# Two-layer graph transformer: layer 1 run over three groups at once, with its transposes taken from TensorE to VectorE and DRAM

## The reference

```
x = layernorm(x + L0(x, adj))     # 8 heads of 48, attention, rmsnorm, SiLU MLP 384-1536-384, rmsnorm
x = layernorm(x + L1(x, adj))     # 12 heads of 32, attention only
L0:  q,k,v = x@wq+bq, x@wk+bk, x@wv+bv
     p = softmax(q k^T * 48**-0.5 + adj);  ctx = p v;  x1 = rms(x + ctx@wo + bo)*alpha1 + gamma1
     out = rms(x1 + silu(x1@w1 + b1)@w2 + b2)*alpha2 + gamma2
```

## Time and profile before

| | us |
|---|---|
| median of 3 runs | 2070.93 (2070.71 to 2072.68) |
| the profiled execution | 2069.64 |
| its span | 2067.8 |
| PE busy | 2028.7 (98%) |
| PE weight loads busy | 1940.5 (94%) |
| DVE busy | 1306.6 (63%) |
| ACT busy | 1137.7 (55%) |
| POOL busy | 514.5 (25%) |

### The profile page before, as it was taken

One profiled execution on the slowest core, in us unless ns is written; L12 is line 12 of the kernel. 1 busy time (PEld: TensorE's weight loads), 2 busy tenths in 40 slices (PEclk: granted clock), 3 DMA queues, 4 the chain that ended last, 5 costly groups with the idle time before them and its releaser, 6 DMA issues.

```text
span 2067.8 us, 46600 instructions
## 1 busy us (share of the span) xinstructions
PE 2028.7 (98%) x16832; PEld 1940.5 (94%) x16832; DVE 1306.6 (63%) x2430; ACT 1137.7 (55%) x2400; POOL 514.5 (25%) x625
## 2 busy tenths in 40 slices
PE   6999999999999999999999999998999999999997
PEld 6999999999999999999999999998899999999997
DVE  6655556655556655556655556655777767776775
ACT  6555555555555555545555555554556555655565
POOL 4223232223232223232223232222122212221221
PEclk9999999999999999999999999999999999999999
DMA  7122121122121121121121121122222222222221
GB/s 215 36 58 54 43 58 43 47 59 52 43 58 43 47 61 50 43 58 43 47 62 48 43 58 43 47 59 78 68 81 84 61 81 82 81 63 81 83 77 63
DMA packets 218876, 129.49 MB, mean 63 GB/s; under 512 B 129888, under 2 KB 217696, under 8 KB 218848
## 3 DMA queue, kind: packets, MB, share of 16 engines
q1 hardware_dynamic: 218848, 129.12, 23.1%
HBM read 78.40 MB, written 37.75 MB: 56 GB/s over the span
## 4 chain that ended last, share of the span: by engine, by line
PE 96%; DVE 2%; ACT 1%; DMA 0%; issue 0%; POOL 0%; SPq 0%; ACTq 0%; POOLq 0%; DVEq 0%
PE a_bank L328 59%; PE b_bank L1092 15%; PE b_banks L1092 5%; PE b_banks L1132 4%; PE a_bank L377 4%; PE b_bank L1155 2%; PE a_bank L404 2%; PE b_banks L1142 2%; PE a_bank L390 1%; PE b_bank L1165 1%; PE a_bank L414 1%; PE a_bank L431 1%; DMA a_work<-in_L_gnn_w 0%; DMA a_work<-in_L_gnn_wq 0%; DVE a_work L705 0%
## 5 line engine op out<-in xcount | busy, mean ns | idle before, releaser
L727 DVE TENSOR_TENSOR a_hid_lo<-a_work,a_hid_hi 128x512 fp32r<-128x512 f32 x192 | 146.6, 763 | 376.7 <-ACT a_hid_hi L573 376.7
L328 PE MATMUL a_bank<-a_x1t_hi,a_w_hi 128*128 128x256 f32 x1152 | 328.1, 285 | 1.5 <-DVE a_x1t_lo L713 1.5
L328 PE MATMUL a_bank<-a_x1t_lo,a_w_hi 128*128 128x256 f32 x1152 | 322.3, 280 | 0.0
L328 PE MATMUL a_bank<-a_x1t_hi,a_w_lo 128*128 128x256 f32 x1152 | 322.0, 280 | 0.0
L568 ACT ACTIVATE a_work<-a_bank,a_b 128x256 f32<-128x256 f32 x384 | 161.1, 472 | 283.5 <-PE a_bank L328 282.3
L919 POOL TENSOR_TENSOR a_work<-a_work,a_gamma 128x384 f32<-128x384 f32 x128 | 150.5, 1197 | 588.4 <-DMA a_work<-in_x 564.0
L328 PE MATMUL a_bank<-a_w_hi,a_hid_hi 128*128 128x384 f32 x768 | 264.1, 344 | 0.5 <-DVE a_hid_lo L727 0.5
L328 PE MATMUL a_bank<-a_w_lo,a_hid_hi 128*128 128x384 f32 x768 | 258.2, 336 | 0.0
L328 PE MATMUL a_bank<-a_w_hi,a_hid_lo 128*128 128x384 f32 x768 | 258.2, 336 | 0.0
L328 PEld LDWEIGHTS a_bank<-a_x1t_hi,a_w_hi 128*128 128x128 f32 x1152 | 217.8, 189 | 5.5 <-DVE a_x1t_lo L713 1.7
L328 PEld LDWEIGHTS a_bank<-a_x1t_lo,a_w_hi 128*128 128x128 f32 x1152 | 217.8, 189 | 0.0
(11 more groups left out here) (157 smaller groups left out, 5698.5 us busy)
## 6 DMA issues: line engine op xcount, KB each, us to landing
a_work<-in_x SPq DMA_DIRECT2D x64, 384.0 KB, 3.4
a_work<-in_xT SPq DMA_DIRECT2D x96, 128.0 KB, 2.6
x2T<-a_z_blocks SPq DMA_DIRECT2D x256, 48.0 KB, 1.7
x<-a_work SPq DMA_DIRECT2D x32, 384.0 KB, 2.7
b_xt_raw<-x2T SPq DMA_DIRECT2D x32, 384.0 KB, 3.5
b_res<-x SPq DMA_DIRECT2D x32, 384.0 KB, 3.8
out<-b_normed SPq DMA_DIRECT2D x32, 384.0 KB, 2.5
b_v_pairs<-b_v_nat SPq DMA_DIRECT2D x128, 49.5 KB, 2.0
```

Of the source, the lines that this page charges most:

```text
L328: r = pe.matmul(out, lhs[a], rhs[b], start=first and n == 0, stop=last and n == 2)
L727: dve.tensor_tensor(hid[1][:, p % RING, :], silu[:, p % 2, :], hid[0][:, p % RING, :].bitcast(F32), ALU.subtract).then_inc(hid_lo, 1)
```

## The change

The layer's step handles three groups instead of two: in step(g), g is new (scores, exp), b = g-1 is back (PV, output projection, x1) and f = g-2 is in the feed-forward; the final norm is of e = g-3. PV of b is issued first on PE, right ahead of the scores of g.

- All 20 PE transposes per group are removed. Instead DVE transposes P, ctx and x1 in 32x32 blocks (turn_p, turn_ctx, turn_x1), SP stores the blocks to a DRAM scratch with eight DMAs of 32 partitions each, and one DMA loads them back in their new place; ACT then makes the hi half (or the copy of P) and DVE the lo half from SBUF.
- exp is written in two pieces per tile into pt, and the copy back from prob to pt is two pieces per tile. The addition of gamma1 goes from POOL to DVE.
- The blocks of ctx, x1 and the output are interleaved so that each SBUF row of a store is 4 runs of 96 values (384 bytes), those of P 4 runs of 128 values (512 bytes). x2T has the same block layout, and the rows of wo, w1 and the second layer's Wq, Wk, Wv are loaded in the order that fits (by_block).
- To make room, w1 is staged in two slots of 512 columns (three pieces) and w2 in two slots of one row block (twelve pieces); eight of the twelve w2 pieces are split in step 0 and four in step 1.
- In the second layer only the layout of its transposed input changes, and its first split (xt_high(0), xt_low(0)) now stands ahead of last["scalar"][0]() and last["vector"][0]().

The core of the diff:

```diff
-            def store(g):
-                for t in range(TILES):
-                    sp.wait_ge(turned, TILES * g + t + 1)
-                    for b in range(P // 32):
-                        sp.dma_start(x2T[g, t, b], z_blocks[32 * b:32 * b + 32, t, :].rearrange("p (k c) -> p k c", c=32)).then_inc(
-                            x2t_stored, 16)
+            def store_p(g, t):
+
+                sp.wait_ge(p_turned, TILES * g + t + 1)
+                for s in range(P // 32):
+                    sp.dma_start(scratch["p"][s, t], prob[32 * s:32 * s + 32, t, :].rearrange("p (u c) -> p u c", u=4)).then_inc(
+                        p_stored, 16)
+
+            def load_pt(g):
+                sp.wait_ge(p_stored, 16 * N_TURNED * (g + 1))
+                sp.dma_start(v["p"], scratch["pt"]).then_inc(pt_loaded, 16)
+
+            def store_blocks(src, dst, t, stored):
+                for s in range(P // 32):
+                    sp.dma_start(dst[P // 32 * t + s], src[32 * s:32 * s + 32, t, :].rearrange("p (m c) -> p m c", m=4)).then_inc(
+                        stored, 16)
+
+            def store_ctx(g, t):
+                sp.wait_ge(ctx_turned, TILES * g + t + 1)
+                store_blocks(blocks, scratch["ctx"], t, ctx_stored)
+
+            def load_ctxt(g):
+                sp.wait_ge(ctx_stored, 16 * N_TURNED * (g + 1))
+                sp.dma_start(turned_raw, scratch["ctxt"]).then_inc(ctxt_loaded, 16)
+
+            def store_x1(g, t):
+                sp.wait_ge(x1_turned, TILES * g + t + 1)
+                store_blocks(blocks, scratch["x1"], t, x1_stored)
+
+            def load_x1t(g):
+                sp.wait_ge(x1_stored, 16 * N_TURNED * (g + 1))
+                sp.dma_start(turned_raw, scratch["x1t"]).then_inc(x1t_loaded, 16)
+
+            def store_x2(g):
                 sp.wait_ge(res_done, TILES * (g + 1))
                 sp.dma_start(x2[g], z).then_inc(x2_stored, 16)
 
+            def store_x2t(g):
+                for t in range(TILES):
+                    sp.wait_ge(z_turned, TILES * g + t + 1)
+                    store_blocks(z_blocks, x2T[g], t, x2t_stored)
+
...
+
+            def load_w2(which):
+                for i in which:
+                    if i >= len(w2_slots):
+                        sp.wait_ge(w2_lo, i - len(w2_slots) + 1)
+                    sp.dma_start(w2_slots[i % len(w2_slots)], w["w2"][i * P:(i + 1) * P, :]).then_inc(
+                        w2_loaded[i % len(w2_slots)], 16)
...
+                if back:
+                    for t in range(TILES):
+                        store_ctx(b, t)
+                if nxt:
+                    load_adj(g + 1)
+                if back:
+                    load_ctxt(b)
...
+                if new:
+                    load_pt(g)
+                if first:
+                    sp.wait_ge(w1_lo, N_W1)
+                if new and (nxt or back):
+                    load_x(g)
+                if first:
+                    load_w2(range(2, 10))
+                if back:
+                    for t in range(TILES):
+                        store_x1(b, t)
+                if late:
+                    store_x2(e)
+                if back:
+                    load_x1t(b)
+                if back and not ffn:
+                    load_w2(range(10, FC))
+                if late:
+                    store_x2t(e)
+                if ffn:
+                    load_res(f)
+                if ffn and not new and back:
...
                 if isinstance(g, int) and g == 0:
                     pe.wait_ge(w_lo, WO + 1)
-                pe.wait_ge(ctxt_lo, TILES * g + t + 1)
                 if t == 0:
-                    pe.wait_ge(ctx_done, TILES * g + 2)
+                    pe.wait_ge(ctxt_lo, g + 1)
+                    pe.wait_ge(ctx_done, TILES * (g + 1))
+                elif new:
+                    pe.wait_ge(biased, TILES * (g + 1) + 1)
...
+            def step(g, new=True, nxt=True, back=True, ffn=True):
+                b, f = g - 1, g - 2
+                if back:
+                    for t in range(TILES):
+                        pv(b, t, new)
+                if new:
+                    for t in range(TILES):
+                        scores(g, t, back)
+                if nxt and not ffn:
                     qk(g + 1)
                 if ffn:
+                    for p in range(3):
+                        ffn1(f, p, new)
                     ffn2(f, 0)
-                    ffn1(f, 2, att)
-                    ffn1(f, 3, att)
+                    ffn1(f, 3, new)
                     ffn2(f, 1)
-                if att:
-                    for t in range(TILES):
-                        turn_p(g, t)
+                    ffn1(f, 4, new)
+                if back:
+                    for t in range(TILES):
+                        attn_out(b, t, new)
                 if ffn:
                     ffn2(f, 2)
-                if att:
-                    for t in range(TILES):
-                        pv(g, t)
-                if ffn:
-                    ffn1(f, 4, att)
-                    ffn2(f, 3)
-                if att:
-                    for t in range(TILES):
-                        turn_ctx(g, t)
-                if ffn:
-                    ffn1(f, 5, att)
-                if att:
-                    for t in range(TILES):
-                        attn_out(g, t)
-                if ffn:
-                    ffn2(f, 4)
-                    ffn2(f, 5)
-
-            step(0, ffn=False)
-            step(1)
-            with pe.Fori(2, NG - 1) as g:
+                    ffn1(f, 5, new)
+                    for p in range(3, FP):
+                        ffn2(f, p)
+                if nxt:
+                    if ffn:
+                        qk(g + 1)
+                    for t in range(TILES):
+                        values(g + 1, t)
+
...
+            def take_pt(g, t):
+                act.wait_ge(pt_loaded, 16 * (g + 1))
+                for s in range(2):
+                    half_t = slice(256 * s, 256 * s + 256)
+                    r = act.activation(pt[:, t, half_t].rearrange("p (h q j) -> p h q j", q=2, j=32),
+                                       prob[:, t, half_t].rearrange("p (q h j) -> p h q j", q=2, j=32), ACT.Copy)
+                r.then_inc(pt_done, 1)
...
+            def ctxt_high(g):
+                act.wait_ge(ctxt_loaded, 16 * (g + 1))
+                wait(act, o_mm, TILES * g)
+                act.activation(ctx_t[0][:].rearrange("p k (n j) -> p k n j", j=32),
+                               turned_raw.rearrange("p (n k j) -> p k n j", k=KT, j=32), ACT.Copy).then_inc(ctxt_hi, 1)
...
+                    for t in range(TILES):
+                        exp(g, t)
+                if first:
+                    high(pieces[WO], w_loaded[WO], 64, w_hi)
+                    for i in range(2):
+                        w1_high(i)
+                if ffn:
+                    hidden(f, 1)
+                if nxt and not first:
+                    split_x(g + 1)
+                if ffn:
+                    hidden(f, 2)
+                    hidden(f, 3)
+                if back:
+                    ctxt_high(b)
+                if not new and ffn and not back:
+                    for i in range(2):
+                        high(next_pieces[i], next_loaded[i], 64, next_hi)
+                if late:
                     variance(e)
                 if ffn:
...
+                    hidden(f, 4)
...
+                if new:
+                    for t in range(TILES):
+                        take_pt(g, t)
+                if back and not second:
+                    x1t_high(b)
+                if nxt:
+                    for u in (1, 2):
+                        take_q(g + 1, u)
+                if first:
+                    w1_high(2)
+                    w2_high(range(0, 8))
+                if second:
+                    w2_high(range(8, FC))
+                    x1t_high(b)
...
+            def turned_low(dst, hi, done, n):
+                dve.wait_ge(hi, n)
+                dve.tensor_tensor(dst[1][:].rearrange("p k (n j) -> p k n j", j=32),
+                                  turned_raw.rearrange("p (n k j) -> p k n j", k=KT, j=32),
+                                  dst[0][:].bitcast(F32).rearrange("p k (n j) -> p k n j", j=32),
+                                  ALU.subtract).then_inc(done, 1)
...
+            def turn_p(g, t):
+                dve.wait_ge(exp_done, TILES * g + t + 1)
+                dve.transpose(prob[:, t, :], pt[:, t, :]).then_inc(p_turned, 1)
+
...
+            def turn_ctx(g, t):
+                dve.wait_ge(ctx_done, TILES * g + t + 1)
+                if t == 0:
+                    wait(dve, x1_stored, 16 * N_TURNED * g)
+                dve.transpose(blocks[:, t, :], ctxt[:, t, :]).then_inc(ctx_turned, 1)
...
+                for t in range(TILES):
+                    dve.wait_ge(x1_scaled, TILES * g + t + 1)
```

(83 more changed lines are left out.)

730 lines of the change are left out of this document (325 added, 405 removed).

## The result

The changed kernel takes 2076.61 us (median of 9 runs, 2075.2 to 2078.24), the kernel before 2071.69 in runs beside it. The ratio is 1.0024, 95% interval 1.0014 to 1.0034: slower by about 5 us. Forecast were 2081 and slower, with a range of 2053 to 2104. The profiled execution's span is 2074.2 us, before 2067.8.

What follows compares the result with a forecast made beforehand. TensorE (PE), busy for 98% of the span, was taken to bound the kernel. From the profile's time, 2069.64 - 70 + 22 + 46 + 13 = 2080.6, forecast as 2081 us; range 2053 to 2104.

Steps and rivals of the forecast that it cites:

- transposes off TensorE: First layer: removing three transposes from TensorE saves 2.19 us a group, 70 us for 32 groups.
- wait for ctx lo: Loop, ahead of attn_out: TensorE waits 0.8 us in 28 steps, 22 us; F is the step's first ffn1 pair's start.
- start: Ahead of the first ffn1, which would start at 110: 46 us more idle, from 33 to 58.
- end and seam: Last two groups and passage to the second layer: waits and half clock together 22 us, 13 more than now.
- second layer: Layer behind the seam: left as it is, no term in the sum.
- Rival 1: Loop at ctx: VectorE's queue is 0.8 shorter, no wait, the 22 goes, 2059 us; chance 0.22.
- Rival 2: Start: 10 to 13 us cheaper than laid out, time about 2069, no change; chance 0.13.
- Rival 3: Loop: VectorE's norm runs beside GpSimd's additions, each step 1.3 longer, 36 us, 2117; chance 0.05.
- Rival 4: DRAM detours: stores and loads take twice as long, 14 us in the loop, 2110 at most; chance 0.15.

Runs made afterwards that it cites:

- experiment 3: Changed kernel with the split of the next x moved behind the split of ctx on ScalarE and VectorE, norm left in place: 2048.15 us, ratio 0.9877.
- experiment 5: Kernel of experiment 3 with twenty extra TensorE transposes per group in one block ahead of attn_out: 2112.91 us, one run.
- experiment 6: Kernel of experiment 3 with twenty extra TensorE transposes per group in three blocks: 2116.18 us, one run.
- experiment 2: Changed kernel with the norm behind ctx's lo half on VectorE, its squares and root behind those of x1 on ScalarE and GpSimd: 2053.15 us, ratio 0.991.
- experiment 4: Changed kernel with eight extra TensorE transposes per group directly ahead of attn_out: 2081.17 us, one run.
- experiment 7: Changed kernel with the first P's return issued ahead of the ten constant loads on SyncE at the start: 2070.82 us, ratio 0.9988.
- experiment 8: Changed kernel with w2 staged in six slots instead of two and the start's pieces and loads reordered: 2053.22 us, ratio 0.9902.
- experiment 9: Kernel of experiment 8 with x(0) loaded early, behind the first two parts of w1: 2049.07 us, ratio 0.9892.
- experiment 1: Changed kernel with the second norm of group e moved behind ctx's lo half on VectorE alone: 2073.11 us, ratio 1.000.
- experiment 12: Kernel of experiments 3 and 9 plus an earlier second-layer first load, with the last group's attn_out ahead of the fifth ffn1 pair: 2012.63 us, ratio 0.9713.

## Why the prediction was right

The sum, in us of span; the measured start is 108.58 - 51.21 = 57.4, less the 13.5 of moved work that the prediction took off.

| term | forecast | measured | from |
|---|---|---|---|
| transposes off TensorE | -70 | -80 | 32 x 2.50, experiment 3 |
| wait for ctx lo | +22 | +27.4 | 28 x 0.98, experiment 3 |
| start | +46 | +44 | first ffn1 |
| end and seam | +13 | +14 | what the other rows leave of the 6.4 |
| second layer | 0 | +0.8 | |
| sum | +11 | +6.4 | spans |

The 2.50 is the loop's value, taken for all 32 groups. The start's 44 takes over the forecast's 13.5 of moved work. TensorE is idle there for 55.5 us against 18.1 before, 37.4 more; the other 6.5 are work at a lower clock. The end's 14 is no measurement of its own. Its rows give 9.7 of idle time and some 5 of slow clock, which agrees to about 1 us; the estimate adds 1.7 and 2.7 for the last two groups and 0.9 for the second layer's first matmuls (8.78 against 7.84).

- *What bounds the kernel, and that TensorE's queue is gained in full:* right, but the sizing was short. The rows of the three transposes gave 2.19 a group; the removal was worth 2.50. This is the term that was mis-sized, by 10 us. The step that failed is "This is the whole gain: projections, scores and PV keep their number and shape". They do, but in their new places they take 0.56 less (experiments 5 and 6), and the transposes, measured by starts, 1.93.
- *The wait at attn_out:* right in place, releaser, count and cause. Forecast / measured, from F: norm starts 11.1 / 11.2, ctx lo starts 14.6 / 14.8, TensorE 15.6 / 15.7. TensorE came 0.1 later than laid out and was free 0.1 earlier (at 14.7), which made 0.98 of 0.8. Experiments 2 and 3 show that split and norm make it together: without the norm 0.16 is left of it, without the split nothing. Experiment 4 shows that 0.87 us of other work on TensorE fit into it.
- *Rival 1* (no wait at ctx) is what experiment 3 makes. It needs 0.9 us, and no closeness of starts gave that. The rival's 2059 would have been 2048 with the right price of the transposes.
- *Rival 2* (a start cheaper by 10 to 13): it was 2 cheaper.
- *Rival 3* (the norm meets GpSimd): not there. The norm's four instructions keep their length, since GpSimd's additions end at F+2.
- *Rival 4* (the detour shows): not in the loop. ScalarE took ctx at F+13.0, SyncE had issued its load at 797.94, F+5.7. The Trainium skill ("DMA: Bandwidth & Descriptors", Specifications) asks for 512 bytes or more for line rate. The time to landing here shows no price for less (1.7 us at 384 bytes); what rate the stores could reach, no run here shows.
- *The start*, forecast / measured: P back 46 / 44.8, ctx(0) 70.4 / 68.1, q and k of group 2 79 / 75.7, end of attn_out 90 / 87.7, first ffn1 110 / 108.6. Experiments 7 to 9 confirm the reasons (constants ahead of P; w2 in two slots ahead of ctx), and that 26 of the 44 are queue order and slots, without telling the two apart.
- *The end*, forecast / measured: waits 4.3 and 5.2 / 3.4 and 4.9, seam 10.2 / 10.3. The slow clock behind them cost more than the 1.3 taken: 54 ffn1 matmuls need 6.4 in the loop and took 8.1 and 9.1. The granted clock was 0.57 over the first 3.9 us behind the first wait, and 0.50 over 3.8 behind the second.

The two mis-sized terms, 10 and 5 us, had opposite signs. That the forecast of 2081 came within 5 us of the time is in part luck.

## What to carry to other kernels

Work taken off the engine that bounds a kernel is gained in full only while the others have slack at the next hand-over: lay out the instructions between what this engine releases and what it next waits for, with their durations, and look which of them do not belong to that hand-over (here a norm and a split, 3 us of 13). When one is moved, move what reads it on every other engine too; experiments 1 and 12 moved one engine's half and got the wait back at another place. What happens once, at the start and the end, can cost more than 32 groups save: 58 us there stood against 53 net in the loop.

## What was not expected of the hardware

Twenty transposes in one block cost 2.02 us, where the three blocks' rows in the kernel before add up to 2.19 and their removal with the new order gave 2.50. The same 12 ffn2 matmuls take 2.08 or 2.25 by what stands ahead of them. Such neighbours are worth half a microsecond a group here, and the rows of the removed instructions don't contain that. And VectorE's subtraction L789 took 1.50 instead of 0.69 when GpSimd's additions ran beside it, as the norm had before the change:

```profile
835.02 1.98 POOL L985 TENSOR_TENSOR a_work<-a_work,a_bo 128x384 f32<-128x384 f32 x2
...
836.06 1.50 DVE L789 TENSOR_TENSOR a_work<-a_work,a_smax 128x512 f32<-128x512 f32 x1
...
838.91 0.69 DVE L789 TENSOR_TENSOR a_work<-a_work,a_smax 128x512 f32<-128x512 f32 x1
```

The meeting that rival 3 feared exists, at another instruction. The second subtraction still ends at 839.60, and the exps start at 840.43, behind ScalarE's own SiLU and table load: in the loop it costs nothing.
